# A routed top-1 expert layer: three groups of tokens instead of two, with first weights fetched per tile

## The reference, cut to what matters

```python
logits = tokens @ Wr + br                       # 2048 tokens, 8 experts
probs = jax.nn.softmax(logits, axis=-1)
expert = jnp.argmax(probs, axis=-1)
max_prob = jnp.take_along_axis(probs, expert[:, None], axis=-1)
h = jax.nn.relu(jnp.einsum('td,edh->teh', tokens, W1) + b1[None])   # 128 -> 256
y = jnp.einsum('teh,ehd->ted', h, W2) + b2[None]                    # 256 -> 128
out = jnp.take_along_axis(y, expert[:, None, None], axis=1)[:, 0, :]
return (out * max_prob).reshape(x.shape)
```

## Time and profile before

| what | value |
|---|---|
| median of 3 runs | 1070.06 us (1069.68 to 1072.22) |
| the profiled execution's own time | 1070.29 us |
| its span, first to last instruction | 1068.5 us |
| TensorE busy | 829.2 us (78%) |
| VectorE busy | 639.4 us (60%) |
| ScalarE busy | 363.8 us (34%) |
| GpSimd busy | 145.8 us (14%) |
| share of TensorE in the chain that ended last | 56% |
| share of VectorE in that chain | 25% |

### The profile page before, as it was taken

How to read it: one execution, slowest core, us unless ns; L and a number is a source line. 1 busy time by engine, 2 the same in 40 slices (tenths; PEclk the granted TensorE clock), 3 DMA queues, 4 the chain that set the end, 5 groups by cost and what they waited for, 6 DMA issues and landing times.

```text
span 1068.5 us, 13018 instructions
## 1 busy us (share of the span) xinstructions
PE 829.2 (78%) x4274; PEld 510.7 (48%) x4274; DVE 639.4 (60%) x2093; ACT 363.8 (34%) x484; POOL 145.8 (14%) x193
## 2 busy tenths in 40 slices
PE   2578899999998997773857474467886678789998
PEld 1123367777776662331736352365564323345554
DVE  6656845444743445754424456877777757767764
ACT  2445544343442345550201120012232355532331
POOL 4010000000000000303051316520010100000000
PEclk9989999999999999885978756686998899899999
DMA  6115300000120101401030100010301111000000
GB/s 162 43 47 197 141 1 1 1 2 1 43 60 1 25 7 33 112 1 40 28 104 20 38 1 0 0 67 1 72 5 26 31 30 30 1 1 10 11 11 10
DMA packets 36876, 37.72 MB, mean 35 GB/s; under 512 B 7284, under 2 KB 32061, under 8 KB 36298
## 3 DMA queue, kind: packets, MB, share of 16 engines
q1 hardware_dynamic: 35786, 34.79, 11.6%
q0 software_dynamic: 1024, 2.10, 0.6%
HBM read 16.47 MB, written 6.03 MB: 21 GB/s over the span
## 4 chain that ended last, share of the span: by engine, by line
PE 56%; DVE 25%; issue 5%; POOL 4%; ACT 4%; SPq 3%; DMA 2%; DVEq 0%; ACTq 0%; POOLq 0%
PE psum_all L643 12%; PE psum_all L623 12%; PE psum_all L673 3%; DVE s_nmx L1097 3%; PE psum_all L655 3%; SPq L2032 3%; PE psum_all L657 3%; PE psum_all L572 2%; PE psum_all L550 2%; DVE s_att L1124 2%; PE psum_all L552 2%; PE psum_all L531 2%; DVE s_x_normed L1009 2%; DVE s_h L1258 2%; PE psum_all L769 2%
## 5 line engine op out<-in xcount | busy, mean ns | idle before, releaser
L1732 ACT ACTIVATE s_hT<-psum_all,s_cols 128x512 f32<-128x512 f32 x160 | 103.0, 684 | 178.4 <-PE psum_all L623 178.3
L1258 DVE SCALAR_TENSOR_TENSOR s_x_resid<-psum_all,s_combine,s_x_resid 128x128 f32<-128x128 f32 x256 | 72.1, 345 | 112.3 <-PE psum_all L643 109.7
L643 PEld LDWEIGHTS psum_all<-s_arena,s_hT 128*128 128x128 f32 x1024 | 123.1, 192 | 31.9 <-issue 30.6
L643 PE MATMUL psum_all<-s_arena,s_hT 128*128 128x128 f32 x1024 | 124.5, 275 | 1.1 <-ACT s_hT L1732 0.6
L623 PE MATMUL psum_all<-s_x_turned,s_arena 128*128 128x512 f32 x256 | 123.2, 604 | 0.0
L1695 ACT ACTIVATE s_hT<-psum_all 77x1024 f32<-77x1024 f32 x96 | 96.4, 1019 | 63.7 <-PE psum_all L552 63.2
L1097 DVE TENSOR_REDUCE s_nmx<-psum_all 128x4 f32<-128x308 f32 x192 | 83.0, 473 | 50.3 <-PE psum_all L531 48.5
L2003 POOL TENSOR_SCALAR s_vare<-s_mv 128x4 f32<-128x4 f32 x40 | 9.2, 229 | 718.5 <-DVE s_mv L1001 718.5
L531 PE MATMUL psum_all<-s_ks,s_t 128*128 128x308 bf16 x192 | 52.4, 326 | 46.5 <-DVE s_nmx L1097 30.1
L550 PE MATMUL psum_all<-s_t,s_ks 128*77 128x512 bf16 x192 | 79.9, 416 | 8.1 <-ACT s_t L1665 4.7
L552 PE MATMUL psum_all<-s_t,s_ks 128*77 128x512 bf16 x192 | 78.7, 410 | 0.0
(11 more groups left out here) (257 smaller groups left out, 1406.6 us busy)
## 6 DMA issues: line engine op xcount, KB each, us to landing
s_t<-s_qparts SPq DMA_DIRECT2D x264, 32.0 KB, 1.9
s_ks<-s_att SPq DMA_DIRECT2D x72, 77.0 KB, 2.1
s_arena<-in_w SPq DMA_DIRECT2D x2, 2048.0 KB, 10.2
s_w<-in_w SPq DMA_DIRECT2D x2, 1024.0 KB, 6.1
sorted_x<-s_arena SPq DMA_DIRECT2D x2, 960.0 KB, 6.5
s_arena<-in_w SPq DMA_DIRECT2D x3, 576.0 KB, 5.0
s_t<-sorted_x SPq DMA_DIRECT2D x6, 256.0 KB, 3.2
sorted_y<-s_arena SPq DMA_DIRECT2D x6, 256.0 KB, 2.3
```

The costliest lines, as they stand in the source:

```text
L643: mm = pe.matmul(PS[:, k, 128 * i:128 * i + 128], hT[:, hs, c, 128 * i:128 * i + 128], w2[L][:, e, c, :], start=(c == 0), stop=(c == NC - 1))
L1258: ins = dve.scalar_tensor_tensor(dst[:, t, :], PS[:, k, 128 * i:128 * i + 128], C[:, t, e:e + 1], dst[:, t, :], ALU.mult, ALU.add)
L1732: ins = nc.scalar.activation(hT[:, n % HS, c, :], PS[:, k + c, :], ACT.Relu if L == 3 else ACT.Gelu, bias=col(f"b1_{L}", NC * e + c))
```

## The change

The 16 tiles are dispatched in three groups: tiles 0 to 7 (blocks 0 and 1), 8 to 11 (block 2) and 12 to 15 (block 3). With 7 spare tiles each that makes 15, 11 and 11 sorted tiles, in 4, 3 and 3 quads: ten quads and 37 tiles, for eight and 30. Group 0 is now normed, routed and ranked in unit (2,2), group 1 in unit (2,3), group 2 among the quads of group 0.

- **Places.** In unit (2,2): norm of block 0 at VectorE's step 0 and of block 1 at step 3, their transposes at TensorE's steps 1 and 5, route at 5, ranking at TensorE's step 6, slots and weights at VectorE's step 6. In unit (2,3): the same for block 2 at 3, 5 and 6. The epilogue in layer 2 goes from (3, 7, 6) to (1, 4, 3).
- **First weights.** W1 of the layer is no longer kept whole on the chip. It lies in device memory as 1024 rows of 258 numbers, 256 weights and two bias columns, and for each sorted tile SP reads the expert's row number into a register and fetches 128 rows (132 KB) into a double buffer, W1R.
- **Hidden layer.** The weights are the stationary operand now and the turned tokens the moving one, in two matmuls per tile. The result comes out already turned, so the second transpose and VectorE's copy are gone, and the bias matmul too. ScalarE's relu takes its bias from the fetched columns, one instruction for each 128 x 128 piece, eight for a quad of four.
- **Registers.** TensorE loads the row numbers of a quad at once, where it loaded them one by one.
- **Queues.** SP goes load, load, then load and store in turn; a load waits for the quad before the last. GpSimd scatters group 0 ahead of the norm of block 2, group 1 ahead of that of block 3, group 2 ahead of layer 4's norm of block 0, and gathers group 0 there, group 1 ahead of that of block 2 and group 2 ahead of that of block 3.
- **Layer 4.** Block 2 starts when group 1's rows are back, block 3 when group 2's are, with the order of `local_layer` rewritten for that.
- **Buffers.** Layer 5 has a value buffer of its own in place of W1's. The other parts of the arena move.

The diff, cut to its core:

```diff
 SORTED_PLACES = {
-    2: {("stats", 0): (0, 1, 0), ("norm", 0): (0, 3, 0), ("front", 0): (4, 0, 5)},
-    3: {("stats", 1): (0, 0, 0), ("norm", 1): (0, 1, 0), ("front", 1): (2, 0, 2), ("R", 0): (3, 3, 4),
-        ("rank", 0): (5, 0, 0), ("slots", 0): (0, 5, 0), ("stats", 2): (0, 7, 0), ("norm", 2): (0, 7, 0)},
+    2: {("stats", 0): (0, 0, 0), ("norm", 0): (0, 0, 0), ("front", 0): (1, 0, 2), ("stats", 1): (0, 3, 0),
+        ("norm", 1): (0, 3, 0), ("front", 1): (5, 0, 5), ("R", 0): (5, 5, 6), ("rank", 0): (6, 0, 0), ("slots", 0): (0, 6, 0)},
+    3: {("stats", 2): (0, 3, 0), ("norm", 2): (0, 3, 0), ("front", 2): (5, 0, 5), ("R", 1): (5, 5, 6),
+        ("rank", 1): (6, 0, 0), ("slots", 1): (0, 6, 0)},
 }
 
 
-EPILOGUE = {0: (3, 7, 7), 1: (3, 8, 7), 2: (3, 7, 6), 6: (3, 6, 7), 7: (3, 8, 8)}
+EPILOGUE = {0: (3, 7, 7), 1: (3, 8, 7), 2: (1, 4, 3), 6: (3, 6, 7), 7: (3, 8, 8)}
 
 
 ATTN, MOE, SORTED, LOCAL, MHA, GLU = "attn", "moe", "sorted", "local", "mha", "glu"
@@ -73,10 +74,29 @@
 GLU_PAIRS = 9
 
 
-HALVES = 2
-HT_TILES = NT // HALVES
-SLOT_TILES = {3: HT_TILES + EXPERTS[3] - 1}
-QUADS = {L: [range(t, min(t + TPB, n)) for t in range(0, n, TPB)] for L, n in SLOT_TILES.items()}
+GROUPS = {3: [(0, 8), (8, 4), (12, 4)]}
+MOST = 8
+SLOT_TILES = {L: [n + EXPERTS[L] - 1 for _, n in groups] for L, groups in GROUPS.items()}
+QUADS = {L: [[range(t, min(t + TPB, n)) for t in range(0, n, TPB)] for n in SLOT_TILES[L]] for L in GROUPS}
...
+            def sorted_hidden(L, g, q):
+                n = quad_no(L, g, q)
+                have(("XT", L, g, q))
+                pe.wait_ge(s_w1[n % 2], 16 * loads(L, n))
+                k = start(("SH", L, g, q), WIDE)
+                for i in range(len(QUADS[L][g][q])):
                     for c in range(2):
-                        mm = pe.transpose(PS[:, k + i // 2, 256 * (i % 2) + 128 * c:256 * (i % 2) + 128 * c + 128],
-                                          HSg[:, n % 2, 256 * i + 128 * c:256 * i + 128 * c + 128], ident)
-                finish(("HT", L, h, q), mm)
-
-            def sorted_values(L, h, q):
-                n = len(QUADS[L]) * h + q
-                have(("HT", L, h, q))
-                k = start(("SY", L, h, q), ACC)
-                for i, t in enumerate(QUADS[L][q]):
+                        mm = pe.matmul(PS[:, k + i // 2, 256 * (i % 2) + 128 * c:256 * (i % 2) + 128 * c + 128],
+                                       W1R[:, n % 2, i, 128 * c:128 * c + 128], XST[:, n % 2, 128 * i:128 * i + 128],
+                                       start=True, stop=True)
+                finish(("SH", L, g, q), mm)
...
+                turn_x, hidden, values = (functools.partial(f, L) for f in (sorted_turn, sorted_hidden, sorted_values))
+                pe.wait_ge(s_w[f"m{L}"], 16)
+                turn_x(0, 0)
+                turn_x(0, 1)
+                hidden(0, 0)
+                hidden(0, 1)
+                values(0, 0)
+                attn_out(L - 1, NB - 1)
+                turn_x(0, 2)
+                values(0, 1)
+                hidden(0, 2)
+                front(L, 3)
+                sorted_route(L, 2)
+                turn_x(0, 3)
+                values(0, 2)
+                hidden(0, 3)
+                sorted_rank(L, 2)
+                turn_x(1, 0)
+                values(0, 3)
+                hidden(1, 0)
+                turn_context()
+                turn_x(1, 1)
+                values(1, 0)
+                hidden(1, 1)
+                turn_x(1, 2)
+                values(1, 1)
+                hidden(1, 2)
+                values(1, 2)
+
+                front(L + 1, 0)
+                turn_x(2, 0)
+                local_scores(L + 1, 0)
+                front(L + 1, 1)
+                hidden(2, 0)
+                turn_x(2, 1)
+                local_scores(L + 1, 1)
+                values(2, 0)
+                hidden(2, 1)
+                turn_x(2, 2)
+                turn_local(L + 1, 0)
+                values(2, 1)
+                hidden(2, 2)
+                turn_local(L + 1, 1)
+                local_context(L + 1, 0)
+                values(2, 2)
+                local_context(L + 1, 1)
+                local_out(L + 1, 0)
+                local_out(L + 1, 1)
...
+                values = functools.partial(sorted_values, L)
                 join_heads(*prev)
                 divide_heads(*prev)
+                values(0, 0)
                 add_out(*prev)
                 front(L, NB - 1)
+                values(0, 1)
+                sorted_route(L, 2)
+                values(0, 2)
+                sorted_slots(L, 2)
+                values(0, 3)
+                sorted_weights(L, 2)
                 window_prep()
+                values(1, 0)
                 gauss_context()
+                values(1, 1)
+                values(1, 2)
+
                 sorted_add(L, 0, range(0, TPB))
                 front_stats(L + 1, 0)
                 sorted_add(L, 0, range(TPB, 2 * TPB))
                 front_apply(L + 1, 0)
                 front_stats(L + 1, 1)
                 front_apply(L + 1, 1)
                 local_scores(L + 1, 0)
+                values(2, 0)
                 local_scores(L + 1, 1)
                 local_probs(L + 1, 0)
+                values(2, 1)
                 local_probs(L + 1, 1)
+                values(2, 2)
+                sorted_add(L, 1, range(2 * TPB, 3 * TPB))
+                front_stats(L + 1, 2)
+                front_apply(L + 1, 2)
                 local_add(L + 1, 0)
                 local_add(L + 1, 1)
+                local_scores(L + 1, 2)
+                sorted_add(L, 2, range(3 * TPB, 4 * TPB))
...
+                    act.wait_ge(*slots.is_made(("SY", L, *quad_at(L, n - 2))))
+                for i in range(len(QUADS[L][g][q])):
+                    for c in range(2):
+                        a = 256 * i + 128 * c
+                        ins = nc.scalar.activation(HTg[:, n % 2, a:a + 128], PS[:, k + i // 2, 256 * (i % 2) + 128 * c:256 * (i % 2) + 128 * c + 128],
+                                                   ACT.Relu, bias=W1R[:, n % 2, i, 256 + c:257 + c])
...
+            def load_quad(g, q):
+                n, some = quad_no(3, g, q), QUADS[3][g][q]
+                m = len(some)
+                if q == 0:
+                    sp.wait_ge(s_te, g + 1)
+                regs = [sp.alloc_register(f"sp_row_{g}_{t}") for t in some]
+                sp.reg_load(regs, tile_expert[0:1, g, some[0]:some[-1] + 1])
+                at = [sp.snap(r, min_val=0, max_val=(EXPERTS[3] - 1) * P) for r in regs]
+                if n >= 2:
+                    sp.wait_ge(*slots.is_read(("SH", 3, *quad_at(3, n - 2))))
+                for i in range(m):
+                    sp.dma_start(W1R[:, n % 2, i, :], A["w1_3"][bass.ds(at[i], P), :]).then_inc(s_w1[n % 2], 16)
+                if q == 0:
+                    sp.wait_ge(s_sc[g], 16 * GROUPS[3][g][1])
+                if n >= 2:
+                    sp.wait_ge(*slots.is_made(("XT", 3, *quad_at(3, n - 2))))
+                sp.dma_start(XS[:, n % 2, 0:m, :], XD[g][512 * q:512 * q + 128 * m, :].rearrange("(t p) d -> p t d", p=P)
+                             ).then_inc(s_xs[n % 2], 16)
+
+            def store_quad(g, q):
+                n, m = quad_no(3, g, q), len(QUADS[3][g][q])
+                sp.wait_ge(*slots.is_read(("SY", 3, g, q)))
+                sp.dma_start(YD[g][512 * q:512 * q + 128 * m, :].rearrange("(t p) d -> p t d", p=P), YS[:, n % 2, 0:m, :]
+                             ).then_inc(s_ys[n % 2], 16)
+
+            sp.wait_ge(s_sel, 1)
+            last = quad_no(3, len(GROUPS[3]) - 1, 0)
+            load_quad(0, 0)
+            load_quad(0, 1)
+            for n in range(last):
+                if n + 2 < last:
+                    load_quad(*quad_at(3, n + 2))
+                store_quad(*quad_at(3, n))
+            load_quad(2, 0)
+            load_quad(2, 1)
+            load_quad(2, 2)
+            for q in range(3):
+                store_quad(2, q)
```

483 lines of the change are left out of this document (201 added, 282 removed).

## The result

The kernel with the change takes 1076.35 us (median of 18 runs, 1071.72 to 1082.78), the kernel before 1071.22 (18 runs, 1067.36 to 1075.16). The ratio is 1.0056, 95% interval 1.0037 to 1.0074: 5 to 6 us slower, where 15 us faster was forecast. The profiled execution has a span of 1074.1 us, before 1068.5.

What follows compares the result with a forecast made beforehand. Bound: TensorE's dispatch waits (20.5, 10.0 and 13.8 us), and in unit (2,2) a tight VectorE. Terms +1.7 - 16.6 - 1.4 = -16.3 from 1070.1 give 1053.8; handoffs worth 1 make 1055 us, range 1036 to 1076.

Steps and rivals of the forecast that it cites:

- Part 1: Unit (2,1), division moved to step 1: it holds up the third max step by 4.5 us; unit 2.8 us longer.
- Part 2: Unit (2,2) with two norms, a route and a ranking, serial on VectorE: +19 us, bounds +10 and +24.
- Rival A: Attention stretch cheaper: unit (2,2) grows by 10 us instead of 19, time 1046 us; chance 0.17.
- Rival B: Clock: unit (2,2), unit (2,3) and the first quads run at 1.2 GHz, +7 us, time 1062; chance 0.13.
- Part 3: Unit (2,3): last values at +24 us against 23.9 now, so zero change; scatters done before norm 2 needs GpSimd.
- rival D: Group 0's rows are not there when attention ends, so the change fails its purpose; time 1072 us; chance 0.02.
- the early dispatch just pays for the routing that it needs, +1.7: Up to the first expert transpose: the 20.5 us wait goes, attention grows, transpose at 508.5 us against 506.8.
- Part 4: Experts and gather: 87.0 us from the first transpose against 103.6, -16.6, of which 10.0 second wait, 5.5 four gather steps.
- The eight relus: ScalarE, experts: eight relus with a bias column take 2.35 us a quad against 1.02, bounds 1.3 and 2.9.
- The loads: SP's weight and row transfers end the wait at quads (0,2), (1,0) and (2,0), by 1 to 2 us each.
- Rival C: SP queue: weight issues of 1.15 to 1.95 us make loads end every quad's wait; slower, 1064 to 1085; chance 0.20.
- Part 5: Layer 4, last routed add to layer 5's first matmul: 36.4 us with one block left, against 37.8; -1.4.

## Why the prediction was wrong, step by step

**Part 1, unit (2,1): +2.8 forecast, +4 measured** (32.0 against 27.9 with the old epilogue). The mechanism was as described; the wait for the third max step is 4.08 us (431.80) where 4.5 was forecast. Slightly under-sized.

**Part 2, unit (2,2): +19 forecast, +22.8 measured**, inside the bounds of +10 and +24. The order laid out on VectorE was right: the third max step ends 19.6 us after the unit's start (19 forecast). The experiments price the pieces: the early epilogue 8.9, of which most is the fourth max step behind the residual add, second norm 8.1, route 3.8, late q and what goes with it some 2. The gap to the forecast opens between the third and the fourth max step. There TensorE's value group, two score pairs and projection were put at 4 us, and VectorE waited 6.03 for them (473.62): the scores come at the slow clock, 0.43 us apart, where the first ones of the unit are 0.21 to 0.25 apart:

```profile
469.74 0.63 PE L571 MATMUL psum_all<-s_t,s_ks 128*77 128x512 bf16 x1
470.17 0.63 PE L573 MATMUL psum_all<-s_t,s_ks 128*77 128x512 bf16 x1
470.59 0.63 PE L571 MATMUL psum_all<-s_t,s_ks 128*77 128x512 bf16 x1
```

So the sum priced most of TensorE's steps at 2.4 GHz where the granted clock was 0.67. How much of the missing 3.8 us that is stays open. Rival A, a unit under 33 us, is refuted. Rival B named the mechanism and put 7 us on it over three stretches. The Trainium skill ("TensorE: Matmul & The Clock Gate", Part 1) calls the slow clock the default that activity lifts; the rise from 0.67 to 0.77 with 32 matmuls more agrees.

**Part 3: zero forecast, +0.8 measured.** Group 0's rows were loaded by SP at 500.16, more than 10 us before the first transpose needed them, so rival D is refuted. The step "the early dispatch just pays for the routing that it needs, +1.7" came out at +9.8 in the profiled executions: 6.4 and 22.8 in the units, 0.8 here, less the wait of 20.5 us (9.5; the rest is the 0.3 by which the stretch begins later).

**Part 4, the experts: -16.6 forecast, -7.1 measured. This is the step that failed most: the relus were priced and left beside TensorE's work, and they stood in its chain.** Its terms:
- The eight relus were sized well (2.35 a quad forecast, 2.2 measured), and then left out of the path: a quad was "0.7 + 1.0 + 2.2 = 4 us" of TensorE, with the relu beside it. The wait table shows them in it, 8.0 us in seven waits, and with one relu a quad the stretch is 86.6 us, where 87.0 was forecast. That near hit is partly luck, since the next two terms were off as well. By the tables of waits it is the order on TensorE that lets the relus into the chain (argued, not tested), and the prediction did not lay that order out for the quads. By the Trainium skill ("ScalarE: Activation LUTs", What ACT_TABLE_LOAD costs) one of them takes 387 ns, and back-to-back ones overlap by some 93: as an estimate from the Trainium skill, 0.29 from one to the next and 2.45 us a quad. The prediction left the overlap out and came to 3.1. The trace is near that estimate, with 0.27 from one to the next and 2.18 for eight (534.76 of ScalarE's timeline).
- The hidden matmuls were priced at 1.0 us by eight transposes of that form. Eight real matmuls are recorded as sixteen and take 2.00 (531.80). This 1 us a quad was not in the forecast 4 us of TensorE either; no run prices it by itself.
- The loads were forecast to end the wait at three quads, 1 to 2 us each, 3 to 6 us in all. They ended one, 1.92 us, and without the fetches the quads gain 0.7. This error of 1 to 4 us offset a part of the second, which is some 9 us over 37 tiles.
- The issue was forecast at 0.62 us and took 0.48. Rival C, the main slower case in the forecast, had the sign right and the reason wrong.

**Part 5, layer 4: -1.4 forecast, +1.6 measured**, and 39.3 to 40.2 in all kernels with three groups against 34.5 to 37.8 in those with two halves. The first transposes behind the last add come 6.2 us after it, where the kernel before has 4.1. The wait of 10.25 us ahead of them (619.27) began before the add, and it is for layer 5's norm of block 0. VectorE applies block 3's norm first:

```profile
615.97 1.11 DVE L1019 TENSOR_SCALAR s_x_normed<-s_x_resid,s_mv,s_rstd 128x128 f32<-128x128 f32 x4 [0.25 <-POOL s_rstd L2014]
...
618.11 1.11 DVE L1019 TENSOR_SCALAR s_x_normed<-s_x_resid,s_mv,s_rstd 128x128 f32<-128x128 f32 x4
```

TensorE, however, has the transposes of layer 5's blocks 0 and 1 and the context of block 2 ahead of block 3's, which come at 627.66, 10.6 us after the norm is done. The forecast had the same order in it. That another order would be shorter is argued from the trace; no run took that part by itself.

**The sum** was off by +8.1 ahead of the experts, +9.5 in them and +3.0 in layer 4, and the rest of the span was 1.3 longer. 1055 + 21.9 = 1076.9, against 1076.35 measured. The largest single piece is that of the relus, priced and not placed in the chain: 7 to 10 us, by the run with one relu.

## What to carry to other kernels

A wait that ends in early dispatch is worth its length less what the early work adds to the stage that takes it; price that stage by laying out its tightest engine in order, and price TensorE's steps there at both clocks, because the unit that began to wait here went from 1.00 to 0.67. See what a step that is moved forward now stands ahead of: the residual add, moved ahead of a max step, made it wait for the output projection. When a producer is cut into short instructions whose consumer needs all of them, look at what the consumer has to do between; in quad (1,1) it was 0.5 us of transposes beside 1.66 to 2.18 us of relus a quad, and the relus came into the chain. Before dispatch is moved to another stage, look at what stands in the queue of the engine that issues it: moving eight scatters ahead of one norm gained 0.5%, and moving them later in front of another lost what it was to bring.

## What was not expected of the hardware

- Eight float32 matmuls of 128x128x128 took 2.00 us where eight transposes of the same shape took 1.04, with a granted clock of 1.00 in both.
- Eight bfloat16 matmuls that close the float32 accumulations of a quad made its hidden layer 0.8 us longer (2.05 to 2.87), 0.1 us each.
- Four transfers with a register in the address were issued in 1.94 us, 0.48 each; the plain ones of the earlier trace rows took 0.59, and the plain loads of sorted rows between them 0.38 to 0.43.
- 32 matmuls added to a unit cost 4.5 us where the clock was 1.00 and TensorE waited for 4.3 us, and 0.3 us where the clock was 0.67 and it waited for 14.4; the clock rose to 0.77.
